# A gated cross-attention block on one Trainium2 core: the masked-key sums read the resident value tiles instead of a second, shifted copy of them

## The chip, the cores and the metric

The kernel runs on one core of one Trainium2 chip, as one launch. The metric is the device time of an execution in microseconds (us). Three executions of the kernel before took 1147.50, 1149.54 and 1154.53 us, median 1149.54 us.

## The reference, cut to what matters

Batch B = 4, S = 512 query rows and SK = 1601 context rows of D = 512 columns each, 16 heads of width 32. After the attention stands a feed-forward part with fp8-rounded operands (width 1408), which the change doesn't touch.

```
x = x + tanh(g_xattn) * mha(layernorm(x), ctx, ctx)
x = x + tanh(g_ffn)   * ffn(layernorm(x))

mha:  scores = q k^T / sqrt(32)
      query i sees key j if j <= i + 1089, otherwise the score is -10000
      out = softmax(scores) v        (v = ctx, k = ctx)
```

A masked key keeps a finite score, -10000. So a row of the output is the ordinary sum over the keys it sees, plus a weight w = exp(-10000 minus the row's maximum) times the plain sum of the value rows that it doesn't see. That plain sum, for every query row, is what the change computes in another way: for query i it is the sum of v[j] over j > i + 1089.

## The kernel before, in words

**Tiling.** The context of one batch is cut into NT = 13 tiles of 128 rows, the last with 65 rows. Queries are QT = 4 tiles of 128. Heads are taken four at a time: NG = 4 groups of GH = 4 heads for each of the 4 batches, so 16 groups in all, `gg` = 0 to 15. `NEAR = SK - S = 1089` is the first key that any query doesn't see. It lies 65 rows into context tile 8 (`DT = 8`), so the four blocks of 128 keys that belong to the four query tiles don't begin where a context tile begins.

**Steps.** A group is worked in STEPS = 26 steps (`u` = 0 to 25), one for each of two pairs of heads and each of 13 context tiles. TensorE (PE) does in every step the scores of the current group (`scores`, L837 and, for tiles that the mask cuts, L843), two steps later the value sums (`values`, L861), and between them one piece of the next group's work: rows of scores for the row maxima (`max_turn`, L780 and L785), which VectorE (DVE) reduces (`max_reduce`, L1064). At fixed steps stand the transposes of keys and queries for the group after next (`stage_turn`, L767 and L759, copied by ScalarE at L592 and split by DVE in `stage_low`, L1055), the output's transposes (`out_turn`), the feed-forward's tiles (`tiles_at`) and, in the first groups, the preparation of the feed-forward weights (`weight_turn`). All engines run through the same list of steps, each in its own program order, and meet through semaphores. Nothing is reordered: an instruction that waits holds up everything behind it on its engine.

**The slots in PSUM.** The jobs of PE that DVE or ScalarE empty (`max`, `stage`, `suf`, `turn`, `up` and others) take turns on two slots of two banks each (`numbered`, L118 to L128). `free_slot` (L737) makes PE wait until the job before the last has been emptied.

**The masked sums.** In each group, at step 6 (`SUMS_AT`), GpSimd (POOL) runs `value_sums` (L478): three instructions that add up whole blocks of 128 value rows into `vsum`. At step 8 (`SUF_AT`) PE runs `suffix_turn` (L797): `later` (ones where key is later than query within a block) times the four blocks `near`, 512 columns, and `onesf` times `vsum`, 384 columns. Both are float32 and each is issued as two halves of 64 output columns (`HALVES`). DVE then weighs the result at L1080 (`suffix_weigh`) into `sw`, and from there `join_out` adds it to the outputs.

**The two copies of the values.** `vf` holds the 13 context tiles of the batch, each head as 32 values and a column of ones, so a head takes 33 elements (`VW`). It is loaded by 13 transfers (`load_values`, L320), each of which waits for the last use of its tile by the batch before (`pv_done`, one tile for each of the last 13 steps), and `values` waits for tile t only when it comes to it. `near` holds rows 1089 to 1600 again, aligned to the queries and without the ones: one transfer of 1 MB per batch (`load_near`, L325), which waits for the last masked sums of the batch before.

**The transfer queue.** SyncE (SP) issues nearly all transfers in a written order (L352 to L410). In the last group of a batch it is: keys, near of the next batch, vf tiles 0 to 3, twelve copies for the first head pair, vf tiles 4 to 7, the row of maxima (`put_shift`, qst<-mrow), vf tiles 8 and 9, twelve copies for the second head pair, and vf tiles 10 to 12. POOL issues only the gathers of weight rows (L415); their descriptors go through a scratch area in the on-chip memory whose size is an argument of `bacc.Bacc` (L1274).

Of the kernel before, what the change touches and what calls it, by code (L numbers as in the profile page):

```python
# [5 lines left out]
def flamingo_gated_block(nc, x_d, ctx_d, gx_d, gf_d, wg_d, wu_d, wd_d, didx_d, out_d):  # L6
    nc.disable_value_cache = True
    f32, f16, bf16, i32 = mybir.dt.float32, mybir.dt.float16, mybir.dt.bfloat16, mybir.dt.int32
    ALU = mybir.AluOpType
# [3 lines left out]
    B, S, D = x_d.shape  # L13
# [150 lines left out]
    with ExitStack() as ctx:  # L164
# [9 lines left out]
        onesf = sb("onesf", [P, P])  # L174
        later = sb("later", [P, P])
        maskT = sb("maskT", [P, P], bf16)
# [14 lines left out]
        vf = sb("vf", [P, NT, H, VW])  # L191
        near = sb("near", [P, QT, H, HD])
        ksrc = sb("ksrc", [P, NT, P])
# [85 lines left out]
        suf_mm, cw_ready, vsum_ready = sem("suf_mm"), sem("cw_ready"), sem("vsum_ready")  # L279
        nmr_ready, nmrf_ready, rows_normed, near_in = sem("nmr_ready"), sem("nmrf_ready"), sem("rows_normed"), sem("near_in")  # L280
        stk = [[sem(f"stk{i}_{r}") for r in range(GH)] for i in range(2)]
# [33 lines left out]
        def load_values(sp, b, t):  # L315
            k0, kn = KT[t]
            if b >= 1:
                last = unit(b * NG - 1, STEPS - NT + t, 1)
                sp.wait_ge(pv_done, last + 1)
            sp.dma_start(vf[0:kn, t, :, 0:HD], ctx_d[b, k0:k0 + kn, :].rearrange("p (h d) -> p h d", h=H)).then_inc(vf_in[t], 16)  # L320

        def load_near(sp, b):
            if b >= 1:
                sp.wait_ge(suf_mm, b * NG)
            sp.dma_start(near[:, :, :, :].rearrange("p t h d -> p t (h d)"),  # L325
                         ctx_d[b, NEAR:SK, :].rearrange("(t p) d -> p t d", p=P)).then_inc(near_in, 16)

# [25 lines left out]
        def _(sp):  # L353
# [13 lines left out]
            put_shift(sp, 0)  # L367
            load_near(sp, 0)
            for o in range(2):
# [5 lines left out]
            for gg in range(GALL):  # L375
# [6 lines left out]
                if gg + 3 < GALL:  # L382
                    load_keys(sp, gg + 3)
                if g == NG - 1 and b + 1 < B:
                    load_near(sp, b + 1)
                if gg >= NG + 1:
# [91 lines left out]
        def value_sums(pool, gg):  # L478

            b, g = divmod(gg, NG)  # L480
            heads = slice(GH * g, GH * g + GH)
            pool.wait_ge(near_in, 16 * (b + 1))
            if gg >= 1:
                pool.wait_ge(suf_mm, gg)
            nc.gpsimd.tensor_copy(vsum[:, 2, :, :], near[:, 3, heads, :]).then_inc(vsum_ready, 1)
            nc.gpsimd.tensor_tensor(vsum[:, 1, :, :], near[:, 2, heads, :], near[:, 3, heads, :], ALU.add).then_inc(vsum_ready, 1)
            pool.wait_ge(vsum_ready, 3 * gg + 2)
            nc.gpsimd.tensor_tensor(vsum[:, 0, :, :], near[:, 1, heads, :], vsum[:, 1, :, :], ALU.add).then_inc(vsum_ready, 1)

# [6 lines left out]
        def _(pool):  # L496
# [13 lines left out]
                                    pattern=[[1, P]], channel_multiplier=-1).then_inc(consts, 1)  # L510
            nc.gpsimd.affine_select(out=later[:, :], in_=onesf[:, :], compare_op=ALU.is_gt, fill=0.0,
                                    base=0, pattern=[[-1, P]], channel_multiplier=1).then_inc(consts, 1)
            nc.gpsimd.affine_select(out=floor[:, :, :], in_=floor[:, :, :], compare_op=ALU.is_gt, fill=-3.0e38,
                                    base=S - 1, pattern=[[-P, QT], [0, GH]], channel_multiplier=-1).then_inc(consts, 1)
            pool.wait_ge(consts, 12)
# [3 lines left out]
            pool.wait_ge(consts, 14)  # L519
# [170 lines left out]
        def _(act):  # L690
            act.wait_ge(consts, 14)
            act.wait_ge(gate_mm, 1)
# [104 lines left out]
        def suffix_turn(pe, gg):  # L797

            job = ("suf", gg)
            b, g = divmod(gg, NG)  # L800
            free_slot(pe, job)
            pe.wait_ge(near_in, 16 * (b + 1))
            pe.wait_ge(vsum_ready, 3 * gg + 3)
            heads, n = slice(GH * g, GH * g + GH), (QT - 1) * P
            for a, e in HALVES:
                nc.tensor.matmul(slot(job)[a:e, 0:S], later[:, a:e], near[:, :, heads, :], start=True, stop=False)
            for a, e in HALVES:
                last = nc.tensor.matmul(slot(job)[a:e, 0:n], onesf[:, a:e], vsum[:, :, :, :].rearrange("p t h d -> p (t h d)"),
                                        start=False, stop=True)
            last.then_inc(suf_mm, 1)  # L810
# [109 lines left out]
        def _(pe):  # L920
            pe.wait_ge(consts, 14)
            pe.wait_ge(gin, 32)
# [265 lines left out]
        def _(dve):  # L1188
            nc.vector.memset(ps[:, 2:4, :], 0.0).then_inc(ps_clear, 1)
            nc.vector.memset(kst[1][ST - 1:ST, :, :], 1.0).then_inc(ones_in[1], 1)  # L1190
            dve.wait_ge(consts, 14)
            s = Steps(dve)
# [91 lines left out]
```

## Time and profile before

| what | value |
|---|---|
| executions | 1147.50, 1149.54, 1154.53 us; median 1149.54 us |
| the profiled execution | 1154.53 us |
| its span in the trace | 1152.8 us |
| mean granted TensorE clock | 0.947 of full speed |
| busy: PE, DVE, ACT, POOL | 83%, 75%, 57%, 27% of the span |

The span is the time from the first to the last instruction of the trace; the execution's time has 1.7 us around it. Busy shares are means over the whole span. "PE" is the matmuls, "PEld" the weight loads that run beside them. In the trace a float32 matmul appears as two records, so the two halves of one product are "x4".

### The profile page before, as it was taken

What the parts mean: (1) busy time and instruction counts of PE and PEld (TensorE: products, weight loads), DVE (VectorE), ACT (ScalarE), POOL (GpSimd) and SP (SyncE); (2) the same over time, 40 slices, a digit from 0 to 9 for tenths busy, and PEclk for the clock granted to TensorE, in tenths of its full rate; (3) what the DMA queues carried; (4) which work ended last, traced back from release to release, by engine and by line L of the source; (5) the groups of instructions that cost most, each with busy time, mean ns of one, the idle gap of its engine ahead of it and who ended that gap; (6) DMA issues with size and microseconds to landing.
All of it is one profiled execution on the core that took longest, in us unless ns stands there. A gap on an engine that the chain in (4) does not pass through costs nothing.

```text
span 1152.8 us, 20968 instructions
## 1 busy us (share of the span) xinstructions
PE 961.7 (83%) x7706; PEld 395.8 (34%) x7706; DVE 863.2 (75%) x1450; ACT 656.1 (57%) x1343; POOL 312.3 (27%) x336
## 2 busy tenths in 40 slices
PE   4598889888889999898889999999799899984444
PEld 2223333333323333343333333333333343432222
DVE  7768789887747878787677878787878776436775
ACT  2165567675646666666556666666556666763322
POOL 3012334333101414132322233231313132433212
PEclk9998899999979999999999999999999999995766
DMA  7952423231672221115812211219421020000000
GB/s 149 150 163 69 116 66 94 66 84 29 146 92 57 66 59 38 55 42 118 127 32 61 72 47 36 57 25 167 80 58 39 19 48 11 2 10 10 10 10 18
DMA packets 157230, 74.87 MB, mean 65 GB/s; under 512 B 111096, under 2 KB 142920, under 8 KB 157128
## 3 DMA queue, kind: packets, MB, share of 16 engines
q1 hardware_dynamic: 155368, 67.77, 27.2%
q0 software_dynamic: 1760, 5.77, 1.8%
q8 instruction: 61, 1.00, 0.4%
q14 instruction: 41, 0.34, 0.1%
HBM read 43.28 MB, written 4.19 MB: 41 GB/s over the span
## 4 chain that ended last, share of the span: by engine, by line
PE 42%; DVE 38%; issue 10%; ACT 4%; POOL 3%; DMA 1%; SPq 0%; DVEq 0%; POOLq 0%; ACTq 0%
DVE mch L1064 18%; PE ps L861 13%; PE ps L837 8%; PE ps L882 6%; PE ps L780 5%; PE ps L905 3%; DVE ff L980 2%; DVE ff L976 2%; DVE ff L984 2%; PE ps L785 2%; ACT pr L632 1%; DVE upd L1107 1%; DVE cmb L1097 1%; PE ps L843 1%; DVE ff L1140 1%
## 5 line engine op out<-in xcount | busy, mean ns | idle before, releaser
L632 ACT ACTIVATE pr<-ps 128x512 f32<-128x512 f32 (+4 forms) x832 | 397.1, 530 | 245.5 <-PE ps L837 127.5
L1064 DVE TENSOR_REDUCE mch<-ps 128x2 f32<-128x1024 f32 (+4 forms) x416 | 433.1, 1056 | 73.8 <-PE ps L785 35.9
L861 PE MATMUL ps<-pr,vf 128*33 128x512 f32 (+4 forms) x1664 | 383.6, 541 | 0.0
L837 PE MATMUL ps<-qst,kst 97*64 97x512 f16 (+4 forms) x1600 | 250.7, 371 | 18.9 <-DMA qst<-mrow 12.2
L780 PE MATMUL ps<-kTh,qTh 32*128 32x512 f16 (+4 forms) x832 | 156.4, 374 | 69.2 <-DVE mch L1064 45.4
L780 PEld LDWEIGHTS ps<-kTh,qTh 32*128 32x128 f16 x832 | 39.5, 91 | 287.3 <-DVE mch L1064 113.3
L837 PEld LDWEIGHTS ps<-qst,kst 97*64 97x64 f16 (+1 forms) x1600 | 77.4, 111 | 109.1 <-ACT pr L632 55.5
L861 PEld LDWEIGHTS ps<-pr,vf 128*33 128x33 f32 (+1 forms) x1664 | 86.9, 113 | 56.6 <-issue 4.8
L1140 DVE SCALAR_TENSOR_TENSOR ff<-ps,scs,wsb 128x352 f32<-128x352 f32 x56 | 32.6, 584 | 70.9 <-PE ps L882 70.9
L882 PE MATMUL ps<-wgu,t_T 128*64 128x352 bf16 x768 | 66.5, 316 | 0.0
L453 POOL TENSOR_TENSOR t_q<-ff 128x768 bf16<-128x768 f32 (+1 forms) x24 | 40.3, 1681 | 95.2 <-DVE ff L984 95.2
L437 POOL TENSOR_TENSOR ff<-ff,wsb 128x352 f32<-128x352 f32 x48 | 45.9, 957 | 64.1 <-DVE ff L1140 64.1
L843 PE MATMUL ps<-maskT,idb 128*64 128x128 bf16 (+2 forms) x576 | 61.9, 215 | 0.0
L1055 DVE TENSOR_TENSOR kTl<-ps,kTh 128x1024 f16<-128x1024 f32 (+1 forms) x32 | 31.6, 990 | 38.7 <-ACT kTh L592 38.6
L458 POOL TENSOR_TENSOR xs<-xs,ff 128x512 f32<-128x512 f32 x14 | 17.8, 1271 | 146.4 <-DVE ff L1184 146.4
L984 DVE TENSOR_TENSOR ff<-ff 128x512 f32<-128x512 f32 (+3 forms) x66 | 55.0, 833 | 2.1
L659 ACT ACTIVATE ff<-ps,scs 128x352 f32<-128x352 f32 x48 | 26.6, 554 | 52.1 <-PE ps L882 52.1
L882 PEld LDWEIGHTS ps<-wgu,t_T 128*64 128x64 bf16 x768 | 44.3, 111 | 32.7 <-issue 20.8
L465 POOL TENSOR_TENSOR xs<-xs,upd 128x256 f32<-128x256 f32 x32 | 23.9, 748 | 109.6 <-DVE upd L1107 109.6
L441 POOL TENSOR_TENSOR ff<-ff 128x352 f32<-128x352 f32 x48 | 51.7, 1078 | 3.8
L492 POOL TENSOR_TENSOR cw<-w,count 128x16 f32<-128x16 f32 x16 | 3.9, 245 | 165.7 <-ACT w L615 165.7
L785 PE MATMUL ps<-idb,maskT 128*64 128x128 bf16 (+2 forms) x640 | 47.2, 230 | 0.0
(149 smaller groups left out, 1169.4 us busy)
## 6 DMA issues: line engine op xcount, KB each, us to landing
kst<-kTh SPq DMA_DIRECT2D x128, 100.1 KB, 2.3
ksrc<-in_ctx SPq DMA_DIRECT2D x16, 768.0 KB
vf<-in_ctx SPq DMA_DIRECT2D x48, 256.0 KB, 5.6
kst<-kTl SPq DMA_DIRECT2D x64, 100.1 KB, 2.3
xs<-in_x SPq DMA_DIRECT2D x16, 256.0 KB, 4.2
qst<-qTh SPq DMA_DIRECT2D x128, 32.0 KB, 2.2
near<-in_ctx SPq DMA_DIRECT2D x4, 1024.0 KB, 6.9
out<-xs SPq DMA_DIRECT2D x16, 256.0 KB, 2.0
```

The costliest lines, as they stand in the source:

```text
L437: nc.gpsimd.tensor_tensor(t_u[e][:, cols], t_u[e][:, cols], wsb[:, I + c * CW:I + (c + 1) * CW], ALU.mult).then_inc(gated, 1)
L441: nc.gpsimd.tensor_tensor(t_u[e][:, cols], t_u[e][:, cols], t_g[e][:, cols], ALU.mult).then_inc(gu_ready, 1)
L632: nc.scalar.activation(pr[0:kn, n % NP, q0:S], ps[0:kn, j, q0:S], ACT.Exp, scale=SCALE).then_inc(ex_done, 1)
L780: last = nc.tensor.matmul(slot(job)[:, 512 * i:512 * i + k1 - k0], qTh[rows, gg % 2, qt * P:(qt + 1) * P], kTh[rows, gg % 2, k0:k1], start ...
L785: last = nc.tensor.matmul(slot(job)[a:e, 512 * i + lo - k0:512 * i + hi - k0], maskT[:, a:e], idb[:, lo - d0:hi - d0], start=False, stop=True)
L837: last = nc.tensor.matmul(ps[a:e, j, q0:S], kst[s][0:ST, r, k0 + a:k0 + e], qst[s][0:ST, r, q0:S], start=True, stop=(t < DT))
L843: last = nc.tensor.matmul(ps[a:e, j, q0:q0 + n_m], idb[:, a:e], maskT[:, m0:m0 + n_m], start=False, stop=True)
L861: nc.tensor.matmul(ps[64 * j:64 * j + VW, 2 + pp % 2, q0:S], vf[0:kn, t, h, :], pr[0:kn, n % NP, q0:S], start=(t == 0), stop=(t == NT - 1) ...
L882: last = nc.tensor.matmul(ps[a:e, bank(job) + side, 0:CW], qxT[:, k, a:e], wgu[:, k, side * I + c * CW:side * I + (c + 1) * CW], start=(k ...
L984: return nc.vector.tensor_tensor(v, v, m, ALU.add)
L1064: nc.vector.tensor_reduce(mch[:, qt, 2 * hp:2 * hp + 2, c], both[:, :, 0:k1 - k0], AX.X, ALU.max).then_inc(dve_free, 1)
L1140: nc.vector.scalar_tensor_tensor(t_g[e][:, cols], ps[:, bank(("up", n, c)), 0:CW], scs[:, n % QT, 1:2], wsb[:, cols], ALU.mult, ALU.mult). ...
```

## The change

- `near`, its load and its semaphore are gone. `vf` is read in its place, by POOL at step 6 and by PE at step 8.
- A block of 128 keys beginning at 1089 + 128 t lies over two context tiles: 63 rows of tile 8 + t and 65 rows of tile 9 + t. So `later` becomes two matrices, one for each, and the product with it becomes two products of 512 columns over tiles 8 to 11 and 9 to 12. The block sums `vsum` are now those of whole context tiles.
- Tile 12 has 65 rows only, and the new products read all 128. POOL therefore clears rows 64 to 127 of it once at the start, and the first load of that tile waits for it.
- POOL and PE wait at the first group of a batch for the vf tiles they read: POOL for tiles 10 to 12, PE for tiles 8 to 12.
- The scratch area for gathers takes its default size instead of 4096.

```diff
-        near = sb("near", [P, QT, H, HD])
-        later = sb("later", [P, P])
+        later = sb("later", [P, 2, P])
...
         def load_values(sp, b, t):
...
+            elif t == NT - 1:
+                sp.wait_ge(tail_zero, 1)
             sp.dma_start(vf[0:kn, t, :, 0:HD], ...).then_inc(vf_in[t], 16)
-        def load_near(sp, b):
-            if b >= 1:
-                sp.wait_ge(suf_mm, b * NG)
-            sp.dma_start(near[...], ctx_d[b, NEAR:SK, :]...).then_inc(near_in, 16)
...
         def value_sums(pool, gg):
-            pool.wait_ge(near_in, 16 * (b + 1))
+            if g == 0:
+                for t in range(NT - 3, NT):
+                    pool.wait_ge(vf_in[t], 16 * (b + 1))
             if gg >= 1:
                 pool.wait_ge(suf_mm, gg)
-            nc.gpsimd.tensor_copy(vsum[:, 2, :, :], near[:, 3, heads, :])
+            nc.gpsimd.tensor_copy(vsum[:, 2, :, :], vf[:, NT - 1, heads, 0:HD])
...
-            nc.gpsimd.affine_select(out=later[:, :], in_=onesf[:, :], ..., base=0, ...)
+            for i in range(2):
+                nc.gpsimd.affine_select(out=later[:, i, :], in_=onesf[:, :], ..., base=i * P - NEAR % P, ...)
...
+            nc.gpsimd.memset(vf[64:P, NT - 1, :, 0:HD], 0.0).then_inc(tail_zero, 1)
+            pool.wait_ge(tail_zero, 1)
             nc.gpsimd.memset(kst[0][ST - 1:ST, :, :], 1.0).then_inc(ones_in[0], 1)
...
         def suffix_turn(pe, gg):
-            pe.wait_ge(near_in, 16 * (b + 1))
+            if g == 0:
+                for t in range(DT, NT):
+                    pe.wait_ge(vf_in[t], 16 * (b + 1))
             pe.wait_ge(vsum_ready, 3 * gg + 3)
             for a, e in HALVES:
-                nc.tensor.matmul(slot(job)[a:e, 0:S], later[:, a:e], near[:, :, heads, :], start=True, stop=False)
+                nc.tensor.matmul(slot(job)[a:e, 0:S], later[:, 0, a:e], vf[:, DT:DT + QT, heads, 0:HD], start=True, stop=False)
             for a, e in HALVES:
-                last = nc.tensor.matmul(slot(job)[a:e, 0:n], onesf[:, a:e], vsum..., start=False, stop=True)
+                nc.tensor.matmul(slot(job)[a:e, 0:n], onesf[:, a:e], vsum..., start=False, stop=False)
+            for a, e in HALVES:
+                last = nc.tensor.matmul(slot(job)[a:e, 0:S], later[:, 1, a:e], vf[:, DT + 1:DT + 1 + QT, heads, 0:HD],
+                                        start=False, stop=True)
...
-    nc = bacc.Bacc("TRN2", target_bir_lowering=False, num_devices=1, dynamic_dma_scratch_size=4096)
+    nc = bacc.Bacc("TRN2", target_bir_lowering=False, num_devices=1)
```

The order of instructions shows what this makes of two places. PE at step 8 of the first group of the second batch, before (L806 and L808 are `suffix_turn`; `vf_in5` and the like are the arrivals of vf tiles):

```order
L861 MATMUL ps<-pr,vf 33x512 [waits ex_done,vf_in5]
L861 MATMUL ps<-pr,vf 33x512 [waits ex_done]
L806 MATMUL ps<-near,later 64x512 [waits vsum_ready,near_in,dve_free]
L806 MATMUL ps<-near,later 64x512
L808 MATMUL ps<-vsum,onesf 64x384 x2
L780 MATMUL ps<-kTh,qTh 128x512 [waits dve_free]
L780 MATMUL ps<-kTh,qTh 128x512
```

and now, with the line numbers of the changed kernel (L863 is the value product, L805, L807 and L810 the masked sums, L777 the next piece of the row maxima):

```order
L863 MATMUL ps<-pr,vf 33x512 [waits ex_done,vf_in5]
L863 MATMUL ps<-pr,vf 33x512 [waits ex_done]
L805 MATMUL ps<-vf,later 64x512 [waits vf_in11,vf_in10,vf_in12,vf_in9,vsum_ready,vf_in8,dve_free]
L805 MATMUL ps<-vf,later 64x512
L807 MATMUL ps<-vsum,onesf 64x384 x2
L810 MATMUL ps<-vf,later 64x512 x2
L777 MATMUL ps<-kTh,qTh 128x512 [waits dve_free]
L777 MATMUL ps<-kTh,qTh 128x512
```

One pair of products of 512 columns is added, and the first of the burst waits for tiles 8 to 12 while the value product just ahead of it waits for tile 5. POOL at step 6 of the same group, before (L485 to L488 are `value_sums`, L465 adds an output into xs):

```order
L465 TENSOR_TENSOR xs<-xs,upd 128x4x64 [waits upd_ready]
L485 COPY vsum<-near 128x128 [waits suf_mm,near_in]
L486 TENSOR_TENSOR vsum<-near 128x128
L488 TENSOR_TENSOR vsum<-near,vsum 128x128 [waits vsum_ready]
L476 TENSOR_TENSOR rstdf<-ve,half 128x4 [waits varf_ready]
```

and now:

```order
L457 TENSOR_TENSOR xs<-xs,upd 128x4x64 [waits upd_ready]
L479 COPY vsum<-vf 128x128 [waits vf_in12,suf_mm,vf_in11,vf_in10]
L480 TENSOR_TENSOR vsum<-vf 128x128
L482 TENSOR_TENSOR vsum<-vf,vsum 128x128 [waits vsum_ready]
L468 TENSOR_TENSOR rstdf<-ve,half 128x4 [waits varf_ready]
```

The same three instructions stand at the same place, but the first now waits for the tile that SP loads last.

## Rows read from the trace of the kernel before

**Rows 1.** The page, part 1: busy time of the two busiest engines.

```profile
PE 961.7 (83%) x7706; PEld 395.8 (34%) x7706; DVE 863.2 (75%) x1450; ACT 656.1 (57%) x1343; POOL 312.3 (27%) x336
```

**Rows 2.** The page, part 4: the chain that ended last, by engine.

```profile
PE 42%; DVE 38%; issue 10%; ACT 4%; POOL 3%; DMA 1%; SPq 0%; DVEq 0%; POOLq 0%; ACTq 0%
```

**Rows 3.** One line, L806: duration in ns min/median/max, starts, shape.

```profile
L806 PE MATMUL ps<-near,later x64: 591/592/643, 78.1 to 999.5; 128*64 128x512 f32 x64
```

**Rows 4.** The chain at step 8 of group 4: start us, us, what.

```profile
338.37 0.86 PE ps L861 x4
339.23 0.86 PE ps L806 x4
340.09 0.65 PE ps L808 x4
```

**Rows 5.** The chain at step 8 of group 7.

```profile
517.22 0.03 DVE ff L984
517.25 0.84 issue
518.10 0.68 DVE sw L1080
518.78 1.13 DVE mch L1064
```

**Rows 6.** Timeline from the same step: start us, us, engine, line, [idle before].

```profile
515.96 0.81 PE L808 MATMUL ps<-vsum,onesf 128*64 128x384 f32 x4
516.71 0.39 PE L780 MATMUL ps<-kTh,qTh 32*128 32x512 f16 x2
...
521.77 1.02 ACT L592 CAST kTh<-ps 128x1024 f16<-128x1024 f32 x1 [0.77 <-PE ps L767]
522.87 1.22 DVE L1055 TENSOR_TENSOR kTl<-ps,kTh 128x1024 f16<-128x1024 f32 x1
523.00 0.09 PEld L780 LDWEIGHTS ps<-kTh,qTh 32*128 32x128 f16 x2 [1.51 <-DVE mch L1064]
```

**Rows 7.** POOL's sums in group 4, timeline.

```profile
334.27 0.29 POOL L485 COPY vsum<-near 128x128 f32<-128x128 f32 x1
335.05 0.46 POOL L488 TENSOR_TENSOR vsum<-near,vsum 128x128 f32<-128x128 f32 x1
```

**Rows 8.** Issues of vf tiles 11 and 12, batches 1 and 3, and time to landing.

```profile
L320 SPq DMA_DIRECT2D vf<-in_ctx x2: 1442/1444/1447, 331.5 to 333.0; - x2
DMA to landing us min/median/max: 5.2/5.2/5.2
...
L320 SPq DMA_DIRECT2D vf<-in_ctx x2: 2042/2351/2660, 820.0 to 822.1; - x2
DMA to landing us min/median/max: 6.3/6.3/6.3
```

**Rows 9.** Timeline at step 8 of group 12.

```profile
826.02 1.08 PE L806 MATMUL ps<-near,later 128*64 128x512 f32 x4
827.75 0.39 PE L780 MATMUL ps<-kTh,qTh 32*128 32x512 f16 x2
830.25 0.68 DVE L1080 TENSOR_TENSOR sw<-ps,w 128x512 f32<-128x512 f32 x1
```

**Rows 10.** Stretches: us, busy PE, PEld, DVE, ACT, POOL, clock, DMA share, GB/s.

```profile
290.00:298.00 8.00, 6.25 (x50) 2.50 (x46) 7.09 (x13) 6.65 (x16) 1.27 (x1) 1.00 1.01 268
...
304.50:313.00 8.50, 8.50 (x64) 2.55 (x60) 6.82 (x9) 5.37 (x12) 0.00 (x0) 1.00 0.36 84
...
317.00:324.00 7.00, 1.50 (x8) 0.60 (x8) 0.12 (x1) 0.82 (x2) 0.00 (x0) 0.54 1.39 146
324.00:331.00 7.00, 7.00 (x34) 2.09 (x34) 2.75 (x3) 3.82 (x8) 0.00 (x0) 0.50 0.67 122
```

**Rows 11.** Waits: engine, line, waited for: us in total, times, longest.

```profile
PE ps L837 <- DMA qst<-mrow: 12.2, 3, 6.3
```

**Rows 12.** POOL's groups by shape: busy us, mean ns, idle before.

```profile
L465 POOL TENSOR_TENSOR xs<-xs,upd 128x256 f32<-128x256 f32 x32 | 23.9, 748 | 109.6 <-DVE upd L1107 109.6
L458 POOL TENSOR_TENSOR xs<-xs,ff 128x512 f32<-128x512 f32 x14 | 17.8, 1271 | 146.4 <-DVE ff L1184 146.4
L415 POOL DMA_INDIRECT ff<-in_L_ffn_w_gate,idx x11 | 10.9, 994 | 3.0 <-POOL t_q L424 2.8 <-POOL t_T L424 0.3
```

**Rows 13.** POOL's start, timeline.

```profile
12.13 1.03 POOL L472 TENSOR_TENSOR rstd<-ve,half 128x4 f32<-128x4 f32 x1 [2.78 <-DVE ve L1020]
```

More of the change, by code:

```diff
@@ L279, in flamingo_gated_block @@
         suf_mm, cw_ready, vsum_ready = sem("suf_mm"), sem("cw_ready"), sem("vsum_ready")
-        nmr_ready, nmrf_ready, rows_normed, near_in = sem("nmr_ready"), sem("nmrf_ready"), sem("rows_normed"), sem("near_in")
+        nmr_ready, nmrf_ready, rows_normed, tail_zero = sem("nmr_ready"), sem("nmrf_ready"), sem("rows_normed"), sem("tail_zero")
         stk = [[sem(f"stk{i}_{r}") for r in range(GH)] for i in range(2)]
@@ L367, in _ @@
             put_shift(sp, 0)
-            load_near(sp, 0)
             for o in range(2):
@@ L383, in _ @@
                     load_keys(sp, gg + 3)
-                if g == NG - 1 and b + 1 < B:
-                    load_near(sp, b + 1)
                 if gg >= NG + 1:
@@ L481, in value_sums @@
             heads = slice(GH * g, GH * g + GH)
-            pool.wait_ge(near_in, 16 * (b + 1))
+            if g == 0:
+                for t in range(NT - 3, NT):
+                    pool.wait_ge(vf_in[t], 16 * (b + 1))
             if gg >= 1:
                 pool.wait_ge(suf_mm, gg)
-            nc.gpsimd.tensor_copy(vsum[:, 2, :, :], near[:, 3, heads, :]).then_inc(vsum_ready, 1)
-            nc.gpsimd.tensor_tensor(vsum[:, 1, :, :], near[:, 2, heads, :], near[:, 3, heads, :], ALU.add).then_inc(vsum_ready, 1)
+            nc.gpsimd.tensor_copy(vsum[:, 2, :, :], vf[:, NT - 1, heads, 0:HD]).then_inc(vsum_ready, 1)
+            nc.gpsimd.tensor_tensor(vsum[:, 1, :, :], vf[:, NT - 2, heads, 0:HD], vf[:, NT - 1, heads, 0:HD], ALU.add).then_inc(vsum_ready, 1)
             pool.wait_ge(vsum_ready, 3 * gg + 2)
-            nc.gpsimd.tensor_tensor(vsum[:, 0, :, :], near[:, 1, heads, :], vsum[:, 1, :, :], ALU.add).then_inc(vsum_ready, 1)
+            nc.gpsimd.tensor_tensor(vsum[:, 0, :, :], vf[:, NT - 3, heads, 0:HD], vsum[:, 1, :, :], ALU.add).then_inc(vsum_ready, 1)
         def masked_count(pool, gg):
@@ L510, in _ @@
                                     pattern=[[1, P]], channel_multiplier=-1).then_inc(consts, 1)
-            nc.gpsimd.affine_select(out=later[:, :], in_=onesf[:, :], compare_op=ALU.is_gt, fill=0.0,
-                                    base=0, pattern=[[-1, P]], channel_multiplier=1).then_inc(consts, 1)
+            for i in range(2):
+                nc.gpsimd.affine_select(out=later[:, i, :], in_=onesf[:, :], compare_op=ALU.is_gt, fill=0.0,
+                                        base=i * P - NEAR % P, pattern=[[-1, P]], channel_multiplier=1).then_inc(consts, 1)
             nc.gpsimd.affine_select(out=floor[:, :, :], in_=floor[:, :, :], compare_op=ALU.is_gt, fill=-3.0e38,
                                     base=S - 1, pattern=[[-P, QT], [0, GH]], channel_multiplier=-1).then_inc(consts, 1)
-            pool.wait_ge(consts, 12)
+            pool.wait_ge(consts, 13)
             nc.gpsimd.tensor_copy(idh[:, :], idf[:, :]).then_inc(consts, 1)
@@ L518, in _ @@
             nc.gpsimd.memset(vf[:, :, :, HD:VW], 1.0).then_inc(vones_in, 1)
-            pool.wait_ge(consts, 14)
+            pool.wait_ge(consts, 15)
             pool.wait_ge(vones_in, 1)
+            nc.gpsimd.memset(vf[64:P, NT - 1, :, 0:HD], 0.0).then_inc(tail_zero, 1)
+            pool.wait_ge(tail_zero, 1)
             nc.gpsimd.memset(kst[0][ST - 1:ST, :, :], 1.0).then_inc(ones_in[0], 1)
@@ L690, in _ @@
         def _(act):
-            act.wait_ge(consts, 14)
+            act.wait_ge(consts, 15)
             act.wait_ge(gate_mm, 1)
@@ L805, in suffix_turn @@
             for a, e in HALVES:
-                nc.tensor.matmul(slot(job)[a:e, 0:S], later[:, a:e], near[:, :, heads, :], start=True, stop=False)
+                nc.tensor.matmul(slot(job)[a:e, 0:S], later[:, 0, a:e], vf[:, DT:DT + QT, heads, 0:HD], start=True, stop=False)
             for a, e in HALVES:
-                last = nc.tensor.matmul(slot(job)[a:e, 0:n], onesf[:, a:e], vsum[:, :, :, :].rearrange("p t h d -> p (t h d)"),
+                nc.tensor.matmul(slot(job)[a:e, 0:n], onesf[:, a:e], vsum[:, :, :, :].rearrange("p t h d -> p (t h d)"),
+                                 start=False, stop=False)
+            for a, e in HALVES:
+                last = nc.tensor.matmul(slot(job)[a:e, 0:S], later[:, 1, a:e], vf[:, DT + 1:DT + 1 + QT, heads, 0:HD],
                                         start=False, stop=True)
@@ L920, in _ @@
         def _(pe):
-            pe.wait_ge(consts, 14)
+            pe.wait_ge(consts, 15)
             pe.wait_ge(gin, 32)
@@ L1190, in _ @@
             nc.vector.memset(kst[1][ST - 1:ST, :, :], 1.0).then_inc(ones_in[1], 1)
-            dve.wait_ge(consts, 14)
+            dve.wait_ge(consts, 15)
             s = Steps(dve)
```

2 lines of the change are left out of this document (removed).

## The prediction

> **What bounds the kernel now.** I read the page's busy times first. PE is busy 83% and DVE 75% of the span [rows 1]: no engine is full, and both are near enough that either may set the pace. The chain that ended last says the same: 42% of it is PE and 38% DVE, transfers have 1% [rows 2]. So the price of a matmul depends on the place. What has to be read is which of the two engines the chain lies on at step 8 of each group, where the masked sums stand.
>
> I followed the chain through that step in all 16 groups. In groups 0, 1, 2, 4 and 15 it runs through the masked sums themselves, as in group 4: value product, 0.86 us of L806, 0.65 us of L808, and on [rows 4]. In group 3 the chain wanders through POOL, but DVE sits idle before L1080 there as in those five, so I count it with them: six groups where PE sets the pace. In groups 5 to 14 it is DVE. There the feed-forward's rounding (L976, L980, L984) stands just ahead of L1080, and the chain shows DVE alone [rows 5]. In group 7 PE is through with L808 and begins the next piece at 516.71, while DVE begins L1080 only at 518.10 [rows 5, 6]: the masked sums are ready 1.4 us before anyone asks for them.
>
> **The change, part by part.**
>
> *The added product.* One pair of float32 matmuls of 512 columns per group. Its twin L806 is the pair on the chain with 0.86 us [rows 4]; every instance has the same length, 591 to 643 ns a record, so the clock was high at all 16 [rows 3]. Cost on PE: 16 x 0.86 = 13.8 us. On the path:
> - Six groups where PE sets the pace: 6 x 0.86 = 5.2 us, in full.
> - Ten groups where DVE does: 0.86 fits into the 1.4 us ahead of L1080, so the chain there is not moved. What comes behind is late, though. PE's key transposes slip by some 0.6 us, ScalarE's copy of them would end not at 522.79 but about 523.4, and DVE's L1055, which began at 522.87, would wait about 0.5 us [rows 6]. The next thing on the chain is L780 at 523.0, which waits for a DVE reduction ahead of L1055 and had 1.51 us of idle time before it [rows 6]. So I take 0 for it, and keep 8 x 0.5 = 4 us as the upper end (in groups 8 and 12 DVE has row statistics in between, which cover it).
>
> *The strided operand.* Both products now read vf in runs of 32 elements with a gap of one, where near gave runs of 128. No row shows PE streaming such an operand. A gain has no reason. For a loss the nearest rows are POOL's: 256 elements in runs of 64 take 748 ns, 2.92 ns each, 512 in one run 1271 ns, 2.48 ns each, so 17% more [rows 12]. That is another engine, so it is an end and no estimate; I take 0, because L808 and L806, of different shapes, both go by their columns alone (0.65 to 0.86 us is 384 to 512) [rows 4]; the upper end is 17% of 1.72 us in 16 groups, 4.7 us. The Trainium skill, "SBUF — State Buffer", section "Door 1: The DMA port swizzle", says the memory is read in lines of 16 bytes and that two hits on a line are enough for full speed; runs of 128 bytes satisfy that, and by that rule the loss is nil. No row here shows it.
>
> *The new waits.* They fall in the first group of batches 1, 2 and 3. POOL's sums at step 6 now need vf tile 12, which SP can issue only after the old batch's last value product (step 1) and which it issues last. In batch 1 tile 11 was issued at 331.5 and landed 5.2 us later, at 336.7; tile 12 was issued 1.5 us behind at 333.0, with half the bytes [rows 8], so I put its landing at 337.4. POOL began its three sums at 334.27 and needs 1.24 us for them [rows 7]: it waits 3.1 us and has them at about 338.8. PE's L806 stands at 339.2 [rows 4]. It is met with 0.4 us to spare, and behind POOL's sums nothing is due for several steps. Batch 2 is alike. In batch 3 the transfers were slower: tile 11 issued at 820.0 and landed at 826.3, tile 12 issued at 822.1 [rows 8], landing about 827.2, sums ready at 828.6. PE wanted to begin at 826.02 [rows 9]. So PE stands 2.6 us, with the rest of its steps queued behind the waiting matmul, and ends the longer burst at 828.6 + 0.86 + 0.65 + 0.86 = 831.0 plus a tail. DVE was busy until its L1080 at 830.25 [rows 9], so it loses about 1.0 us, not 2.6. Term: 1.0 us. Lower end 0 (the transfer lands as in batch 1), upper end 3 x 2.6 = 7.8 us.
>
> *The load of near.* Four transfers of 1 MB go. Their time is hidden: the one at 290 falls in a stretch with a DMA share of 1.01, but by 304.5 to 313 the share is down to 0.36 [rows 10], and the transfer that PE does wait for, qst<-mrow, comes at 318. What stands in front of that one are the vf tiles, and they stay. Taken as 0; the gain if I am wrong is the third rival.
>
> *The rest.* One more mask and one clearing on POOL at the start lie ahead of L472, which waited 2.78 us for DVE anyway [rows 13]; two instructions of that size fit. The first load of tile 12 waits for a clearing at the very start, long before SP comes to that load. The larger scratch: the gathers take 994 ns each with next to no spread and 3.0 us of idle time in all [rows 12], and none shows a wait for room. Taken as 0, and nothing to gain.
>
> **The sum.** 5.2 + 1.0 = 6.2 us. The profiled execution would go from 1154.53 to 1160.7 us. It was the slowest of three; the same 6.2 us on the median of 1149.54 gives 1155.7, and I say **1156 us**.
>
> **The rivals.**
>
> *All sixteen groups pay.* If DVE's late L1055 in groups 5 to 14 isn't absorbed, or PE is really the limit and the chain's DVE share is an accident of its rule for following, the price is 13.8 + 1.0 us and 1164 us; with the strided operand's end 1169 us. For it: PE's 83%. Against it: the 1.4 us between burst and L1080 [rows 5, 6].
>
> *The new wait bites and takes the clock.* If POOL's sums come late in each of three batches, PE stands 2.6 us each time. The trace shows what standing can do: PE busy 1.50 us of 7 between 317 and 324, granted clock 0.54, and then seven full microseconds at 0.50, the lower level of 1.2 GHz [rows 10]. Work of 7 us at half speed costs 3.5 us. One boundary that goes so adds 2.6 + 3.5 us for a total of 1161 us; three give 5.2 + 18.3, 1173 us. Against it: the wait would be much shorter than the 6.3 us one that went ahead of that drop [rows 11]. The Trainium skill, "TensorE: Matmul & The Clock Gate", section "HAM oscillation — how this bites in real kernels", has an idle PE throttled and then working cold; by that rule batch 3 with its 2.6 us is the place at risk.
>
> *Faster: the 1 MB load was what made qst<-mrow late.* PE waited 12.2 us for it at three boundaries [rows 11], and after the first ran at half clock for some 7 us of full work [rows 10]. If near's traffic were what pushed the vf tiles and with them mrow back, taking it out would give 12.2 + 3.5 = 15.7 us; less the 6.2 that is 1140 us. It decides where the queue hasn't drained by the time of the copies at 304: against it speaks the share of 0.36 between [rows 10].
>
> **How the numbers follow.** My forecast (1150 to 1160) has a chance of 0.60; all groups pay 0.20; wait and clock 0.12; the load was in the way 0.08. A measurement of this kernel can tell about 1%, 11.5 us, from no change. Of the first case nearly everything is within 1%; of the second and third about two thirds lie beyond 1161; of the fourth about two thirds are faster by over 1%. That gives faster 0.05, same 0.73, slower 0.22. The range: the low end lets in a little of the fourth case and three executions that spread over 7 us, 1147; the high end the second with its strided end, 1169.
>
> **What would show it.** In the profile of the changed kernel: L805 and L810 as pairs of 0.86 us; in groups 5 to 14 L1080 still right behind L984 without idle time; PE idle before L805 in group 12 by 2 to 3 us, in groups 4 and 8 by less than 0.5; POOL idle for vf some 3 us three times; mrow's waits still near 12 us; the clock's mean within 0.01. I am wrong if L806's successor takes more than 1 us a pair, if DVE is idle before L1080 in groups 5 to 14, if the waits for mrow shrink by several us, or if drops of the clock stand behind the new waits.

## The result, and the profile after

The changed kernel takes 1157.67 us (median of 5 runs, 1155.66 to 1158.47), the kernel before 1149.54 us (5 runs, 1147.50 to 1154.53). The ratio is 1.0066, with a 95% interval of 1.0038 to 1.0094: 7.6 us slower (4.4 to 10.8). The ratio is that of the means, so a difference in us taken from a ratio (ratio times 1149.5) can be apart from the difference of the medians, here 8.1 us. The forecast was 1156 us, 6.2 us slower.

The busy times of the page, in answer to [rows 1], and the chain's shares, in answer to [rows 2]:

```profile
PE 969.0 (84%) x7770; PEld 399.7 (35%) x7770; DVE 862.0 (75%) x1450; ACT 656.3 (57%) x1343; POOL 312.9 (27%) x338
...
PE 42%; DVE 38%; issue 11%; ACT 4%; POOL 3%; DMA 1%; SPq 0%; POOLq 0%; DVEq 0%; ACTq 0%
```

PE has 64 records more, the 32 new products. It is busy only 7.3 us longer, though 13.8 us of work were added, and the span grew by 0.6 us only, from 1152.8 to 1153.4. Part of the reason is in the clock. The profiled execution of the kernel before was the slowest of its five (1154.53 us), and the changed kernel's took 1155.15 us, less than any of its timed ones. The drops of the clock lie at different places in the two. Two stretches of groups 8 and 12 ran at the lower level only in the kernel before, and 6.8 us at the start of group 12 only in the changed one. The columns are those of [rows 10]; first the kernel before, then the changed one:

```profile
590.60:594.00 3.40, 3.40 (x22) 1.04 (x18) 3.24 (x8) 1.06 (x4) 1.02 (x1) 0.50 0.00 0
836.30:839.70 3.40, 3.40 (x26) 1.30 (x22) 3.09 (x8) 1.00 (x3) 0.69 (x1) 0.51 0.00 0
809.60:816.40 6.80, 5.74 (x62) 3.20 (x64) 3.59 (x5) 4.54 (x9) 2.03 (x2) 1.00 0.93 138
```

```profile
590.60:594.00 3.40, 3.29 (x33) 1.22 (x34) 3.37 (x10) 1.67 (x5) 0.52 (x1) 1.00 0.02 5
836.30:839.70 3.40, 1.73 (x15) 0.59 (x16) 3.40 (x5) 1.73 (x3) 1.53 (x1) 1.00 0.00 0
809.60:816.40 6.80, 5.87 (x40) 2.95 (x40) 1.77 (x3) 2.56 (x5) 1.06 (x2) 0.50 1.08 134
```

So the two spans must not be subtracted. What can be compared is what happens inside a stretch that has the same clock in both. The answer to [rows 3], and who waited, from the changed kernel's view of L805 and of L810:

```profile
L805 PE MATMUL ps<-vf,later x64: 591/592/643, 76.9 to 1000.3; 128*64 128x512 f32 x64
  POOL vsum L482: 1.3, 1
L810 PE MATMUL ps<-vf,later x64: 592/592/592, 78.4 to 1001.8; 128*64 128x512 f32 x64
  DVE sw L1082: 13.1, 6
```

The records of both products have the 592 ns of [rows 3]: reading vf in runs of 32 costs nothing. And DVE waits for L810 at six places, 13.1 us in all. They are groups 0 to 4 and 15, the very groups in which the prediction had PE set the pace.

Group 7 in the changed kernel, the timeline that answers to [rows 5, 6]:

```profile
518.30 1.08 PE L805 MATMUL ps<-vf,later 128*64 128x512 f32 x4
519.21 0.81 PE L807 MATMUL ps<-vsum,onesf 128*64 128x384 f32 x4
519.86 1.03 PE L810 MATMUL ps<-vf,later 128*64 128x512 f32 x4
520.47 0.96 DVE L986 TENSOR_TENSOR ff<-ff 128x768 f32<-128x768 f32 x1
521.35 0.68 DVE L1082 TENSOR_TENSOR sw<-ps,w 128x512 f32<-128x512 f32 x1
...
526.60 1.23 DVE L1057 TENSOR_TENSOR kTl<-ps,kTh 128x1024 f16<-128x1024 f32 x1 [0.39 <-ACT kTh L589]
```

DVE's L1082 stands right behind L986 as before, 3.05 us after the start of the burst in both kernels, while the burst is 0.86 us longer. L1057 waits 0.39 us, where 0.5 was expected. Two groups earlier the same instruction began at 397.64 before and 400.88 after:

```profile
397.64 0.68 DVE L1080 TENSOR_TENSOR sw<-ps,w 128x512 f32<-128x512 f32 x1
```

```profile
400.88 0.68 DVE L1082 TENSOR_TENSOR sw<-ps,w 128x512 f32<-128x512 f32 x1
```

The distance is 3.24 us in group 5 and 521.35 - 518.10 = 3.25 us in group 7. Two groups with their added product added nothing, and the 0.39 us was absorbed as well. From group 9 to group 11 it is the same: -0.40 and -0.38 us.

The new wait shows in group 4. The chain of the changed kernel there, and PE's timeline:

```profile
335.09 4.74 DMA vf<-in_ctx
```

```profile
339.08 1.03 PE L863 MATMUL ps<-pr,vf 128*33 128x512 f32 x4
341.40 1.08 PE L805 MATMUL ps<-vf,later 128*64 128x512 f32 x4 [1.29 <-POOL vsum L482]
```

PE stands 1.29 us, where the prediction had it met with 0.4 us to spare. In group 8 it stands too, for 1.67 us. The view puts that down to DVE's reduction, which freed the slot, but POOL's last sum ended only at 582.55, so without that reduction PE would have stood nearly as long:

```profile
582.12 0.43 POOL L482 TENSOR_TENSOR vsum<-vf,vsum 128x128 f32<-128x128 f32 x1
...
582.69 1.08 PE L805 MATMUL ps<-vf,later 128*64 128x512 f32 x4 [1.67 <-DVE mch L1066]
```

In group 12, where the prediction had PE stand 2.6 us, it doesn't wait: POOL got tile 12 after 3.10 us and had its sums before PE came at 828.37.

```profile
827.01 0.29 POOL L479 COPY vsum<-vf 128x128 f32<-128x128 f32 x1 [3.10 <-DMA vf<-in_ctx]
...
828.37 1.08 PE L805 MATMUL ps<-vf,later 128*64 128x512 f32 x4
```

PE, not the transfer, had changed. The group's first scores began at 810.54 in the kernel before and at 810.53 in the changed one, and PE came to the masked sums at 826.02 and at 828.37. Between the two lies the stretch at 809.60 to 816.40 shown above, at half clock in the changed kernel only.

### The profile page after: what moved, and what is told of

Same layout as the page of the kernel before. It is cut to its first block, busy times and chain, and to the rows that moved or that the text cites. A ratio compares the mean times of both kernels' runs of the same rounds, so it can differ in the third digit from the quotient of the medians.

```text
span 1153.4 us, 21093 instructions
## 1 busy us (share of the span) xinstructions
PE 969.0 (84%) x7770; PEld 399.7 (35%) x7770; DVE 862.0 (75%) x1450; ACT 656.3 (57%) x1343; POOL 312.9 (27%) x338
## 4 chain that ended last, share of the span: by engine, by line
PE 42%; DVE 38%; issue 11%; ACT 4%; POOL 3%; DMA 1%; SPq 0%; POOLq 0%; DVEq 0%; ACTq 0%
DVE mch L1066 18%; PE ps L863 12%; PE ps L839 8%; PE ps L884 6%; PE ps L777 5%; PE ps L907 3%; DVE ff L982 2%; DVE ff L978 2%; DVE ff L986 2%; PE ps L782 2%; ACT pr L629 1%; DVE upd L1109 1%; DMA qst<-mrow 1%; DVE cmb L1099 1%; PE ps L845 1%
## 5 line engine op out<-in xcount | busy, mean ns | idle before, releaser
L863 PE MATMUL ps<-pr,vf 128*33 128x512 f32 (+4 forms) x1664 | 379.8, 536 | 0.0
L839 PE MATMUL ps<-qst,kst 97*64 97x512 f16 (+4 forms) x1600 | 250.6, 371 | 17.7 <-DMA qst<-mrow 11.2
L777 PE MATMUL ps<-kTh,qTh 32*128 32x512 f16 (+4 forms) x832 | 156.0, 373 | 60.0 <-DVE mch L1066 40.9
L777 PEld LDWEIGHTS ps<-kTh,qTh 32*128 32x128 f16 x832 | 39.5, 91 | 277.9 <-DVE mch L1066 106.9
L863 PEld LDWEIGHTS ps<-pr,vf 128*33 128x33 f32 (+1 forms) x1664 | 86.9, 113 | 57.1 <-issue 5.5
L1057 DVE TENSOR_TENSOR kTl<-ps,kTh 128x1024 f16<-128x1024 f32 (+1 forms) x32 | 31.6, 991 | 40.7 <-ACT kTh L589 40.7
L450 POOL TENSOR_TENSOR xs<-xs,ff 128x512 f32<-128x512 f32 x14 | 17.8, 1272 | 143.9 <-DVE ff L1186 143.9
L986 DVE TENSOR_TENSOR ff<-ff 128x512 f32<-128x512 f32 (+3 forms) x66 | 55.0, 833 | 2.1
```

What stands on the lines that cost most here:

```text
L777: last = nc.tensor.matmul(slot(job)[:, 512 * i:512 * i + k1 - k0], qTh[rows, gg % 2, qt * P:(qt + 1) * P], kTh[rows, gg % 2, k0:k1], start ...
L839: last = nc.tensor.matmul(ps[a:e, j, q0:S], kst[s][0:ST, r, k0 + a:k0 + e], qst[s][0:ST, r, q0:S], start=True, stop=(t < DT))
L863: nc.tensor.matmul(ps[64 * j:64 * j + VW, 2 + pp % 2, q0:S], vf[0:kn, t, h, :], pr[0:kn, n % NP, q0:S], start=(t == 0), stop=(t == NT - 1) ...
L986: return nc.vector.tensor_tensor(v, v, m, ALU.add)
```

## The experiments

Theory A: the product costs its 0.86 us in the six groups where PE sets the pace (0 to 4 and 15) and nothing where DVE does; the new waits are a small term beside it; the missing load, the strided read and the scratch area are nothing. Its rivals: all sixteen groups pay and something else gives back; or the waits carry the loss. "Before" in a ratio is always the kernel before, timed on the same chip.

**p1, the product alone**, in the kernel before:

```diff
             for a, e in HALVES:
-                last = nc.tensor.matmul(slot(job)[a:e, 0:n], onesf[:, a:e], vsum..., start=False, stop=True)
+                nc.tensor.matmul(slot(job)[a:e, 0:n], onesf[:, a:e], vsum..., start=False, stop=False)
+            for a, e in HALVES:
+                last = nc.tensor.matmul(slot(job)[a:e, 0:S], zer[:, a:e], near[:, :, heads, :], start=False, stop=True)
```

> The kernel before, with one more pair of float32 products of 512 columns per group (near times an all-zero matrix, so the sums stay the same) and nothing else of the change. Theory A (the price is paid where PE sets the pace, groups 0 to 4 and 15, and hidden behind DVE in groups 5 to 14): 6 x 0.86 = 5.2 us over the kernel before, ratio 1.0045; DVE's weighing in groups 5 to 14 starts without idle time. Theory B (all sixteen groups pay, and other parts of the change give some back): 13.8 us, ratio 1.012.

Measured: 1156.17 us, ratio 1.0057 (1.0041 to 1.0073), 6.6 us (4.7 to 8.4). Theory B's 1.012 lies outside; theory A's 1.0045 inside. DVE waits for the added product in groups 0 to 4 and 15 and nowhere else. The product alone is most of the change's loss, and by these intervals it can be all of it.

**p2, the waits alone**, in the kernel before:

```diff
         def value_sums(pool, gg):
             pool.wait_ge(near_in, 16 * (b + 1))
+            if g == 0:
+                for t in range(NT - 3, NT):
+                    pool.wait_ge(vf_in[t], 16 * (b + 1))
...
         def suffix_turn(pe, gg):
             pe.wait_ge(near_in, 16 * (b + 1))
+            if g == 0:
+                for t in range(DT, NT):
+                    pe.wait_ge(vf_in[t], 16 * (b + 1))
```

> The kernel before, still computing from near, but with the change's waits: POOL for vf tiles 10 to 12 and PE for tiles 8 to 12 in the first group of a batch. Theory A (product and waits are separate terms that add up to the measured 8 us; in the changed kernel's trace the chain stands on the transfer of tile 12 in group 4 and PE idles 1.3 us there): 1.5 to 3 us, ratio 1.001 to 1.003, PE idle before its masked sums in group 4 by 1 to 1.5 us. Theory B (the waits are hidden as forecast for two batches of three and cost 1 us in the last): at most 1 us, and idle time in group 12 rather than in group 4.

Measured: 1148.97 us, ratio 1.0006 (0.9986 to 1.0026): 0.7 us, between -1.6 and 3.0. The time can't tell the two apart. The view of waits shows theory A's place: PE stood in group 4 and in no other.

```profile
334.88 1.08 PE L812 MATMUL ps<-near,later 128*64 128x512 f32 x4 [1.30 <-POOL vsum L491]
```

**p9, both together**, the edits of p1 and p2 in the kernel before.

> The kernel before with the product of p1 and the waits of p2 together, still computing from near. What it lacks of the change is the read of vf, the missing load and the larger scratch area. Theory A (nothing else costs or gives): the sum of p1's and p2's, 6 to 9 us over the kernel before, ratio 1.005 to 1.008, as the changed kernel. Theory B (the strided read of vf costs, or the missing load gives): apart from the changed kernel by more than 2 us.

Measured: 1155.97 us, ratio 1.0064 (1.0044 to 1.0084), and the changed kernel has 1.0066. What p9 lacks of the change (vf read instead of near, no load, the larger scratch area) is together nothing that can be measured; the two intervals allow some 2 us either way. Where PE stands differs from execution to execution, though: here it stood 1.35 us in group 4 and 1.00 us in group 12.

**p10 and p11, the two parts that should be nothing.** p10 is the changed kernel with `load_near` back at its old places and nobody reading what it loads; p11 the changed kernel with `dynamic_dma_scratch_size=4096`.

> The changed kernel with the four 1 MB transfers into near put back at their old places, unread (scratch area 4096 to make room). Theory A (the transfers were hidden): within 1.5 us of the changed kernel, ratio to before 1.005 to 1.008, first wait for mrow at the boundaries as in the changed kernel. Theory B (the missing load gave something back, which covers a dearer product): 3 us or more over the changed kernel.

> The changed kernel with the gathers' scratch area at 4096 again. Theory A: no change, within 1.5 us of the changed kernel, ratio to before 1.005 to 1.008, gathers at 0.96 to 1.0 us each. Theory B (the larger area gives something back): 3 us or more over the changed kernel.

Measured: 1156.20 us, ratio 1.0067 (1.0047 to 1.0087), and 1157.54 us, ratio 1.0070 (1.0047 to 1.0094). Both are the changed kernel's 1.0066. PE waited 11.3 us for mrow in p10, 11.2 us in the changed kernel: 1 MB more per batch in the queue didn't move it. In p10 PE stood for POOL's sums in all three places, 1.36, 0.45 and 0.72 us.

p11 differs from the changed kernel in the size of the scratch area only, and its profiled execution shows something that the changed kernel's did not: a longer stall in group 8, and a drop of the clock behind it (the stretches have the columns of [rows 10]).

```profile
582.42 1.33 PE L805 MATMUL ps<-vf,later 128*64 128x512 f32 x4 [2.38 <-POOL vsum L482]
583.48 1.55 PE L807 MATMUL ps<-vsum,onesf 128*64 128x384 f32 x4
584.75 1.94 PE L810 MATMUL ps<-vf,later 128*64 128x512 f32 x4
```

```profile
580.00:582.40 2.40, 0.04 (x2) 0.01 (x1) 2.40 (x4) 1.46 (x3) 1.14 (x3) 1.00 0.01 1
582.40:586.00 3.60, 3.58 (x12) 1.28 (x12) 1.83 (x3) 0.00 (x0) 1.62 (x1) 0.60 0.00 0
```

**p4, the product twice.** The changed kernel with a third product, by zeros (and the small scratch area, as in p3, p7, p8 and p10; p11 shows no cost of it).

```diff
             for a, e in HALVES:
-                last = nc.tensor.matmul(..., later[:, 1, a:e], vf[:, DT + 1:DT + 1 + QT, heads, 0:HD], start=False, stop=True)
+                nc.tensor.matmul(..., later[:, 1, a:e], vf[:, DT + 1:DT + 1 + QT, heads, 0:HD], start=False, stop=False)
+            for a, e in HALVES:
+                last = nc.tensor.matmul(..., zer[:, a:e], vf[:, DT + 1:DT + 1 + QT, heads, 0:HD], start=False, stop=True)
```

> The changed kernel with yet another pair of products of 512 columns per group (an all-zero matrix; scratch area 4096 to make room). The burst on PE becomes 3.45 us, DVE comes to the weighing 3.05 us after its start in groups 5 to 7, 9 to 11, 13 and 14, so 0.4 us shows there; in groups 8 and 12 (4.2 us) nothing. Theory A: 6 x 0.86 + 8 x 0.4 = 8.4 us over the changed kernel, ratio to before 1.014. Theory B (all sixteen pay always): 13.8 us over the changed kernel, ratio 1.019. Theory C (the pair's price on the chain is less than its length because other waits take it up): under 6 us, ratio under 1.012.

Measured: 1166.20 us, ratio 1.0149 (1.0130 to 1.0169), 8.5 us over the changed kernel's median and 9.5 us by the ratios, where 8.4 was worked out. Theory B's 1.019 and theory C's 1.012 lie outside. The room ahead of DVE's weighing is now used up, and what sticks out of it shows as DVE's idle time in group 7:

```profile
528.23 1.03 PE L815 MATMUL ps<-vf,zer 128*64 128x512 f32 x4
529.31 0.69 DVE L1087 TENSOR_TENSOR sw<-ps,w 128x512 f32<-128x512 f32 x1 [0.36 <-PE ps L815]
```

The expected 0.4 us is there. DVE waited for L815 at 15 places (all but group 12), and for L810 at 6 in the changed kernel.

**p3, a second set of tiles 8 to 12.** The changed kernel with tiles 8 to 12 of odd batches in five tiles of their own, so that they can be loaded early, at the place in SP's order where near was loaded:

```diff
+        def vt(b, t):
+            return t + (NT - DT) * (b % 2) if t >= DT else t
...
             for gg in range(GALL):
...
+                if g == NG - 1 and b + 1 < B:
+                    for t in range(DT, NT):
+                        load_values(sp, b + 1, t)
```

> The changed kernel with a second set of vf tiles 8 to 12 for odd batches, loaded at the place where near was loaded, so that the new waits find their data (scratch area 4096 to make room). Theory A: gains back the waits' term, 1.5 to 3 us under the changed kernel, so 5 to 6.5 us over the kernel before, ratio 1.0045 to 1.0055, no idle time of PE on vf. Theory B (the rest of the 8 us lies elsewhere, in late L1055 or in the transfers' order): no gain, 8 us over the kernel before.

Measured: 1167.52 us, ratio 1.0149 (1.0130 to 1.0168), 10 us slower than the changed kernel. Neither theory had that. The waits on vf at the boundaries are gone, but another has grown:

```profile
PE ps L840 <- DMA qst<-mrow: 21.2, 3, 7.8
```

mrow is the row of maxima, which PE needs for the first scores of a group. It had cost 12.2 us in the kernel before [rows 11] and 11.2 in the changed one, and it comes late when more vf tiles are issued in the same group. That made two questions: what p3 would show without this (p7), and what the kernels would take if mrow were not late (p5, p6, p8).

**p7, the second set loaded one group earlier** (`g == NG - 2` in the lines above).

> As p3 (a second set of vf tiles 8 to 12 for odd batches), but they are loaded one group earlier, so that nothing is put ahead of mrow at the boundary. In p3 the wait for mrow grew from 11 to 21 us and hid the question. Theory A: mrow's waits at about 10 to 12 us again, no idle time on vf, 0 to 3 us under the changed kernel, ratio to before 1.004 to 1.007. Theory B (the second buffer itself or its traffic costs): as p3, ratio 1.012 or more.

Measured: 1155.43 us (12 runs), ratio 1.0040 (1.0021 to 1.0060). PE waited 11.0 us for mrow, and POOL for vf in the first group of the launch only. The expectation of theory A is met, at its lower end. That mrow's wait is back at 11 us shows that the five tiles issued in the same group had made it grow in p3. Without the new waits the loss is 4.6 us, against 7.6 with them; the intervals overlap, so the 3 us between them are not shown by these two alone.

**p5, mrow first**, in the kernel before:

```diff
                 if gg + 2 < GALL:
                     sp.wait_ge(dve_free, dve_count["stage", gg + 2, 0])
                     put_heads(sp, gg + 2, 0)
-                if g == NG - 1 and b + 1 < B:
-                    for t in range(4, 8):
-                        load_values(sp, b + 1, t)
                 if gg + 1 < GALL:
                     put_shift(sp, gg + 1)
+                if g == NG - 1 and b + 1 < B:
+                    for t in range(4, 8):
+                        load_values(sp, b + 1, t)
```

> The kernel before with one change in the transfer queue: at a batch boundary the row of maxima (qst<-mrow) is issued ahead of vf tiles 4 to 7 instead of behind them. Theory A (PE's three waits for mrow, 12.2 us in the kernel before, come from the four vf transfers issued just ahead; p3 made them 21.2 us by issuing more): the waits go to under 2 us, and the clock's long drop at the first boundary with them, 12 to 16 us under the kernel before, ratio 0.986 to 0.990. Theory B (mrow is late because of the chain of maxima itself, the queue has no part): no change.

Measured: 1131.94 us, ratio 0.9830 (0.9806 to 0.9853), 19.5 us faster by the ratio and 17.9 us by the medians, where 12 to 16 was expected. An estimate from the trace of the kernel before comes near it: 12.2 us of waits, half of the 8.5 us that PE worked at about half clock after the first of them [rows 10], and half of the 3.40 us in the stretch after the second, 18.2 us in all, without the drops in groups 8 and 12 shown above. p5 has none of these: its granted clock is 1.00 from 290 to 1010 us.

```profile
563.30:566.70 3.40, 3.40 (x28) 1.81 (x26) 0.13 (x1) 1.22 (x3) 0.00 (x0) 0.50 1.28 164
```

Why mrow was late shows in the kernel before, too. ScalarE had written the row of maxima at 313.06, as SP turned to the four vf tiles, and SP took 5.21 us to issue them:

```profile
312.50 0.56 ACT L608 COPY mrow<-ps 4x512 f16<-4x512 f16 x1
```

```profile
312.96 5.21 SPq L320 DMA_DIRECT2D vf<-in_ctx  x4
318.22 1.88 SPq L345 DMA_DIRECT2D qst<-mrow  x1
```

On SP's queue the copy from mrow now stands ahead of the vf tiles (start, length, line, count):

```profile
312.99 0.64 SPq L345 DMA_DIRECT2D qst<-mrow  x1
313.68 9.81 SPq L320 DMA_DIRECT2D vf<-in_ctx  x6
```

No wait for mrow is left, and PE goes through the first boundary at full clock, where the kernel before had the two lower rows of [rows 10]:

```profile
317.00:324.00 7.00, 6.92 (x48) 2.24 (x46) 4.62 (x10) 5.20 (x10) 0.61 (x1) 1.00 1.30 130
324.00:331.00 7.00, 7.00 (x46) 2.15 (x46) 5.68 (x7) 3.26 (x6) 1.22 (x4) 1.00 0.84 134
```

**p6, mrow first**, the same edit in the changed kernel.

> The changed kernel with the same edit in the queue. In the kernel before nobody needs vf tile 12 until step 14; here POOL needs it at step 6. From the issue of mrow to tile 12's landing SP needs 6 vf transfers, twelve copies and 3 more vf transfers, some 24 us; PE needs some 15 us to step 8. Theory A (the new waits are hidden only because PE stands for mrow first): PE stands for vf tile 12 about 5 to 8 us at each of the three boundaries, so that the edit gives only 0 to 4 us under the changed kernel, ratio to before 1.002 to 1.007. Theory B (waits and mrow are separate): the edit gives what it gives to the kernel before.

Measured: 1166.88 us, ratio 1.0130 (1.0106 to 1.0155): the edit that gave the kernel before 19.5 us costs the changed one 9 us by the medians, 7 us by the ratios. The direction is theory A's, but it went further than its 1.002 to 1.007. The waits, and PE's timeline at the first boundary:

```profile
POOL vsum L479 <- DMA vf<-in_ctx: 45.1, 4, 14.6
PE ps L805 <- POOL vsum L482: 26.9, 3, 11.0
```

```profile
329.88 1.03 PE L863 MATMUL ps<-pr,vf 128*33 128x512 f32 x4
341.94 1.97 PE L805 MATMUL ps<-vf,later 128*64 128x512 f32 x4 [11.03 <-POOL vsum L482]
```

and the stretches around it, columns as in [rows 10]:

```profile
330.00:342.00 12.00, 0.97 (x8) 0.10 (x3) 1.47 (x2) 0.95 (x2) 1.14 (x3) 0.71 0.63 93
342.00:349.00 7.00, 7.00 (x38) 2.40 (x40) 2.87 (x4) 1.83 (x4) 0.00 (x0) 0.77 0.00 0
```

PE comes to the masked sums early and then stands 11.0 us, 9 us on the mean of three. I had expected 5 to 8. The clock falls behind it, as it fell behind mrow's wait before. The 11.2 us of waits for mrow have turned into 26.9 us of waits for tile 12.

**p8, mrow first and the second set**, the edits of p5 and p7 in the changed kernel.

> p7 and the edit of p5 together: the changed kernel with neither the wait for tile 12 nor the wait for mrow. Theory A: it gains what p5 gains over the kernel before and keeps only the product's price of 5 to 7 us: 6 to 10 us under the kernel before, ratio 0.991 to 0.995. Theory B: ratio above 1.

Measured: 1136.50 us, ratio 0.9871 (0.9848 to 0.9894), 14.8 us faster than the kernel before. 6 to 10 us had been expected, because p5's gain had been put too low. With the new waits out of the way the edit gives nearly what it gives there, and p8, like p5, shows no drop of the clock from 290 to 1010 us. Against p5 the ratio is 0.9871 / 0.9830 = 1.0042, and 1136.50 - 1131.94 = 4.6 us: the product's price once more, with 5.2 worked out.

| kernel | us | ratio to before |
|---|---|---|
| changed | 1157.67 | 1.0066 |
| p1 product alone | 1156.17 | 1.0057 |
| p2 waits alone | 1148.97 | 1.0006 |
| p9 product and waits | 1155.97 | 1.0064 |
| p7 changed, no wait for the tail | 1155.43 | 1.0040 |
| p10 changed, near loaded but unread | 1156.20 | 1.0067 |
| p11 changed, small scratch area | 1157.54 | 1.0070 |
| p4 changed, product twice | 1166.20 | 1.0149 |
| p3 changed, second set in the boundary group | 1167.52 | 1.0149 |
| p5 before, mrow first | 1131.94 | 0.9830 |
| p6 changed, mrow first | 1166.88 | 1.0130 |
| p8 changed, mrow first, no wait for the tail | 1136.50 | 0.9871 |

p5 is the fastest of them.

## Why the prediction was right, point by point

- **The added product, 5.2 us.** Right, and shown. Alone it costs 6.6 us (4.7 to 8.4), and between p5 and p8 4.6 us. The reading behind it holds too: six places where DVE waits for the burst, none in groups 5 to 14, and the distance between the kernels doesn't change from group 5 to group 7 or from 9 to 11. p4 tested the margin itself: once the burst is longer than 3.05 us, nine of the ten hidden groups show DVE waiting, by what sticks out.
- **The late L1055, 0.** Right: 0.39 us late and absorbed.
- **The strided operand, 0.** Right: 592 ns a record, as for near. The Trainium skill, "SBUF — State Buffer", section "Door 1: The DMA port swizzle", has two hits on a line of 16 bytes as enough for full bandwidth; by that rule runs of 128 bytes lose nothing, and the trace agrees.
- **The new waits, 1.0 us, in batch 3.** The size can't be told from the measured 0.7 us (-1.6 to 3.0), and the place was wrong, so that the term is of the right order is luck. PE stood 1.3 us in group 4, in the changed kernel and in p2, and not in group 12. Two steps failed. In group 4 it was the landing of tile 12, carried over from one execution with a margin of 0.4 us. The group's first scores give both kernels a common mark, first in the kernel before, then in the changed one:

```profile
322.50 1.06 PE L837 MATMUL ps<-qst,kst 97*64 97x512 f16 x4 [6.26 <-DMA qst<-mrow]
```

```profile
323.70 1.06 PE L839 MATMUL ps<-qst,kst 97*64 97x512 f16 x4 [5.55 <-DMA qst<-mrow]
```

From that mark PE came to the masked sums after 16.6 us before and 16.4 us in the changed kernel, nearly the same. Tile 12 was issued after 10.5 us before (333.0) and after 11.4 us in the changed kernel (335.09), and took 4.74 us to land where 4.4 had been assumed. So the margin was lost on SP, which came 0.9 us later to the issue; why it did stays open. In group 12 the failed step was to take PE's arrival from an execution that ran there at full clock. From the first scores PE came after 15.5 us before and after 17.8 us in the changed kernel, behind 6.8 us at half clock, while POOL had its sums after 17.7 us. With 15.5 us PE would have stood 2.2 us, as an estimate. Group 8 of the changed kernel is such a case: no drop, PE there after 15.5 us, the sums after 17.1. A margin below a microsecond between a queue and an engine with a varying clock is none.
- **The load of near, 0, and the larger scratch, 0.** Right, as far as can be measured: p10 and p11 both stand at the changed kernel's ratio, with intervals of 2 us either way.
- **The sum.** 6.2 us forecast, 7.6 us measured (4.4 to 10.8). The 5.2 us in it rest on a mechanism that the runs show; the 1.0 us do not.
- **All sixteen groups pay (0.20).** Refuted by p1.
- **The new wait bites and takes the clock (0.12).** Not what carries the loss: no drop of the clock stands behind the stalls of 1.29 and 1.67 us in the changed kernel's profiled execution. But it can happen in as good as the same kernel. In p11's execution a stall of 2.38 us in group 8 has a stretch with a granted clock of 0.60 behind it. At full size it shows in p6: 26.9 us of stalls and the clock at 0.71 and 0.77. Where PE came late to step 8, held up by a drop behind mrow's wait, the new wait did not bite; what it costs on average was not separated from the product, and lies between nothing and some 3 us.
- **Faster, the load of near made mrow late (0.08).** Refuted by p10, which keeps the load and has the same waits for mrow. The half of it that said the queue makes mrow late was right, only that the vf tiles do it: the prediction named them, took them as given and didn't price them. Their price is 18 to 19.5 us, more than twice the change under study. The waits for mrow were 21.2, 11.3 and 0 us in p3, p10 and p5, by how many vf tiles SP issues ahead of it in that group. Part of it is SP's own time, 5.21 us for four tiles at the first boundary, with the row of maxima ready. The Trainium skill, "DMA: Bandwidth & Descriptors", section "Queues, rings and completion order", says that each DMA engine consumes the descriptors of one issuer's ring in ring order; by that rule the small transfer also starts behind the descriptors of the vf tiles in its ring. The three runs agree with it, but don't separate it from SP's time.

## What to carry to other kernels

An engine at 83% doesn't make each of its instructions cost its length: follow the chain through every instance of the place that is changed, count those where it runs through the engine, and measure at the others the gap to whoever uses the result. Before merging a second copy of data into a buffer that is refilled in place, look not only whether the new reader's wait is met today, but what it is met by. Here it was met, or nearly, because another stall came first, and the merged version could then no longer gain from removing that stall.

## What the runs showed that I had not expected

- Four vf transfers issued ahead of one of 4 KB cost 12.2 us of waits at three boundaries and 18 to 19.5 us of time, the rest for the most part through the clock, which falls behind the stalls. One transfer moved in the queue's order takes all of it away.
- The same transfer moved in the changed kernel makes it 7 to 9 us slower: 11.2 us of waits become 26.9 us of other waits.
- More work can leave the span nearly alone in a single profile. With 13.8 us added on PE the two profiled spans differ by 0.6 us, while the medians differ by 8.1. Drops of the clock fall at different places in the two: stretches of 3.4 us in groups 8 and 12 in one execution, one of 6.8 us at the start of group 12 in the other.
- A stall that one profiled execution doesn't show can stand in the next. In group 8 PE didn't stand in p9, where the clock had dropped behind mrow's wait and PE came 18.3 us after its first scores; it stood 2.38 us in p11, where no drop had come before and it was there after 15.5 us.
